# The output bias in a two-layer graph attention kernel: from a matmul to an addition on GpSimd

## The chip, the cores and the metric

The kernel runs on one core of a Trainium2 chip. The metric is device microseconds per execution, the median of three runs. The engines are TensorE (PE; its weight loads are listed as PEld), VectorE (DVE), ScalarE (ACT), GpSimd (POOL) and SyncE (SP), which issues every DMA here. Each engine takes its instructions in the order of its own program and stops at the first whose semaphore has not been reached.

## The reference, cut to what matters

128 graphs of 128 nodes with 512 features go through two layers. Layer 0 is cosine-gated graph attention with 8 heads, and its output is x1. Layer 1 is masked attention with 4 heads of 64, then an output projection with a bias and a residual:

```python
    h = jnp.maximum(_layernorm(x, axis=-1), 0.0)
    x = x + _L0_gnn_ref(h, adj, ...)                 # x1 in the kernel
    h = jnp.maximum(_layernorm(x, axis=-1), 0.0)
    x = x + _L1_gnn_ref(h, adj, ...)                 # ends in: return out @ Wo + bo
```

So the result of a graph is x1 + out @ Wo + bo, with bo (512 values, not zero) the same for all its rows. It must come out in fp32.

## The kernel before, in words

All matrix products are done on fp16 pairs: a value is split into an upper fp16 part (written by ScalarE) and a lower one (the difference, mostly made by GpSimd, some by VectorE). Products are three passes: upper by upper, upper by lower, lower by upper. Projections of layer 0 go over two graphs at a time.

Time is divided into slots, one per graph, and every engine has a function `slot(s)` that lists its work of that slot; odd and even slots differ, so the work repeats every two slots (a pair, in which two graphs are finished). The order is written out by hand, the loops are unrolled, and semaphores alone connect the engines. In slot n the kernel works on graph n of layer 0, graph n-4 and n-3 of layer 1, and the output of graph n-5. The names that the prediction uses:

- POOL, odd slot: `h1_lower` (line 571), `squares_last` (631), `keep_and_block` (618, 625), `x_lower` (602, twice), `o1_lower` (577), `q_lower` (609), `inverse_norms` (a power, 637, and two copies, 643), `q_lower`, `e_lower` (588), `directions_lower` (650, twice), `norm_l1` (659 to 664), `o1_lower`.
- POOL, even slot: `h1_lower`, `v_lower` (594, twice), `keep_and_block`, `p1_lower` (583), `e_lower`, `p1_lower`, `norm_l1`, `norm_l0`.
- SyncE, odd slot: `turn_h1`, two small loads, `turn_x` (transposes what `x_lower` completes, 500, twice), `load_x` (509, twice), `turn_o1` (438, transposes the attention output o_hl into o_t), the two halves of `turn_e`, `store` (490).
- ScalarE, odd slot, after the exponentials: `o1_upper` for the second graph (813), which overwrites o_hl and so waits until `turn_o1` has landed, then the upper part of the first half of k (821), of lq, and `directions_upper` (838, twice), and later the second half of k (821).
- VectorE, odd slot: `k_lower` (966, the lower part of k, both inputs in SBUF), lq's lower part (991), `directions` (1039, twice), the second half of k, `result` (1084).
- PE: in an odd slot `scores`, `cosines`, the projections q, k, lq, lk, the sums, and `output` before lk; in an even slot `scores`, `cosines`, the layer-1 scores, the projections m, the sums, `output`, then v and lv.

`scores` of the next slot waits for `k_lower` of the second half of k, and `cosines` for `directions_lower`. The output is a PSUM bank that PE fills with the bias first, and VectorE scales and adds to x1:

```python
nc.tensor.matmul(ps, three_rows[:, :], bias_y[:, :], start=True, stop=False)
rows(ps, w_o, o_t, first=False).then_inc(proj_full, 1)
```

Here three_rows is 128x128 with ones in rows 0, 32 and 64, and bias_y holds bo over the output scale as a sum of three bf16 parts in those rows, prepared once by eight instructions of GpSimd.

Of the kernel before, what the change touches and what calls it, by code (L numbers as in the profile page):

```python
# [30 lines left out]
BF16 = mybir.dt.bfloat16  # L31
# [8 lines left out]
P = 128  # L40
# [88 lines left out]
def wait(engine, sem, count):  # L129

    if isinstance(count, int) and count <= 0:
        return
    engine.wait_ge(sem, count)
# [21 lines left out]
def build(nc, x, adj, map_w, map_b, q_w, q_b, k_w, k_b, gcn_map_w, gcn_map_b, gcn_W, Wq, Wk, Wv, Wo, bo, out):  # L155
# [13 lines left out]
    with ExitStack() as ctx:  # L169
        def sb(name, shape, dt=F32):  # L170
            return ctx.enter_context(nc.sbuf_tensor(name, shape, dt))

        def sem(name):
            return ctx.enter_context(nc.semaphore(name))
# [9 lines left out]
        w_o = [sb(f"w_o_{s}", [P, C1, D], F16) for s in ("hi", "lo")]  # L184

        ident = sb("ident", [P, P])
        three_rows = sb("three_rows", [P, P], BF16)
        bias_y = sb("bias_y", [P, D], BF16)
        head_sel = sb("head_sel", [P, C, H], BF16)
        minus_half = sb("minus_half", [P, 2 * H])  # L190
        largest = sb("largest", [P, NAMED])
# [5 lines left out]
        v_unscale = sb("v_unscale", [P, 2])  # L197
        v_unkept = sb("v_unkept", [P, 1])
        y_scale = sb("y_scale", [P, 1])
        y_unscale = sb("y_unscale", [P, 1])  # L200
        col_map_b = sb("col_map_b", [P, C])
        col_qb = sb("col_qb", [P, C])
        col_kb = sb("col_kb", [P, C])
# [171 lines left out]
        p1_done = sem("p1_done")  # L375
        dir_hi = sem("dir_hi")
        dir_lo = sem("dir_lo")
        bias_step = sem("bias_step")
        settled_sp = sem("settled_sp")
        settled_pool = sem("settled_pool")  # L380
        settled_dve = sem("settled_dve")
# [18 lines left out]
                + [("gcn", None, 0)] + [("split", w_v, c) for c in range(C)] + [("bias_v", None, 0)]  # L400
                )
        SMALL_LOADS = 7
        ONES = 9
        L_AT = 2 * C
        TURNED_K = 3 * C + 1 + C
        BIAS_K = TURNED_K + C + 1
# [132 lines left out]
        def _(pool):  # L539
# [11 lines left out]


            pool.wait_ge(consts, 7)
            nc.gpsimd.memset(three_rows[:, :], 0.0).then_inc(ones_in, 1)
            nc.gpsimd.memset(lv_sb[:, 0, :, :, DH:DH + 1], 1.0).then_inc(ones_in, 1)
            nc.gpsimd.memset(lv_sb[:, 1, :, :, DH:DH + 1], 0.0).then_inc(ones_in, 1)
            pool.wait_ge(ones_in, 3)
            for part in range(3):
                nc.gpsimd.memset(three_rows[32 * part:32 * part + 1, :], 1.0).then_inc(ones_in, 1)
            pool.wait_ge(ones_in, 6)  # L560
            pool.wait_ge(largest_done, 1)
            nc.gpsimd.partition_all_reduce(top[:, 0:1], largest[:, 0:1], P, RED.absmax).then_inc(top_done, 1)
            pool.wait_ge(largest_done, NAMED)
# [3 lines left out]
            def h1_lower(s):  # L567
                if s.has(-2):
                    pool.wait_ge(h1_hi, s.at(lambda t: t - 2 + 1))
                    a = s.n % 2  # L570
                    nc.gpsimd.tensor_tensor(h1_hl[:, a, 1, :], h1_sb[:, a, :], h1_hl[:, a, 0, :],  # L571
                                            ALU.subtract).then_inc(h1_lo, 1)

            def o1_lower(s, behind):
                if s.has(-behind):
# [52 lines left out]
            def squares_last(s):  # L628
                if s.has(1):
                    pool.wait_ge(sq_rest_done, s.at(lambda t: (t + 1) // 2 + 1))  # L630
                    nc.gpsimd.tensor_tensor(sq_parts[2], sq_rest[:, :, :], sq_parts[1], ALU.subtract).then_inc(sq_last_done, 1)
# [47 lines left out]
            def slot(s):  # L679
                if s.odd:  # L680
                    h1_lower(s)
                    squares_last(s)
                    keep_and_block(s)
                    x_lower(s)
                    o1_lower(s, 5)
                    q_lower(s, 0)
                    inverse_norms(s)
                    q_lower(s, 1)
                    e_lower(s)
                    directions_lower(s, 0)  # L690
                    directions_lower(s, 1)
                    norm_l1(s)
                    o1_lower(s, 4)
                else:
                    h1_lower(s)
                    v_lower(s)
                    keep_and_block(s)
                    p1_lower(s, 4)
                    e_lower(s)
                    p1_lower(s, 3)  # L700
                    norm_l1(s)
                    norm_l0(s)

            early_slots(B, slot)
            pool.wait_ge(scale_done, 2)
            nc.gpsimd.tensor_scalar(bias_o[:, :], bias_o[:, :], y_unscale[:, :], None, ALU.mult).then_inc(bias_step, 1)
            pool.wait_ge(bias_step, 1)
            nc.gpsimd.tensor_copy(bias_y[:, :], bias_o[:, :]).then_inc(bias_step, 1)
            pool.wait_ge(bias_step, 2)
            nc.gpsimd.tensor_tensor(ybuf[:, 0, :], bias_o[:, :], bias_y[:, :], ALU.subtract).then_inc(bias_step, 1)  # L710
            pool.wait_ge(bias_step, 3)
            nc.gpsimd.tensor_copy(bias_y[32:64, :], ybuf[32:64, 0, :]).then_inc(bias_step, 1)
            nc.gpsimd.tensor_copy(bias_y[64:128, :], ybuf[64:128, 0, :]).then_inc(bias_step, 1)
            pool.wait_ge(bias_step, 5)
            nc.gpsimd.tensor_tensor(ybuf[64:128, 1, :], ybuf[64:128, 0, :], bias_y[64:128, :], ALU.subtract).then_inc(bias_step, 1)
            pool.wait_ge(bias_step, 6)
            nc.gpsimd.tensor_copy(bias_y[64:128, :], ybuf[64:128, 1, :]).then_inc(ones_in, 1)
            pool.wait_ge(ones_in, 7)
            pool.wait_ge(prep_copied, BIAS_K)
            nc.gpsimd.memset(v_sb[:, 0, :, :, DK:DK + 1], 1.0).then_inc(ones_in, 1)  # L720
            nc.gpsimd.memset(v_sb[:, 1, :, :, DK:DK + 1], 0.0).then_inc(ones_in, 1)
# [174 lines left out]
        def _(dve):  # L896
# [182 lines left out]
            def result(s):  # L1079
                if s.has(-5):  # L1080
                    u = s.proj("wo")
                    dve.wait_ge(proj_full, u.full)
                    wait(dve, y_out, s.at(lambda t: 16 * (t - 6)))
                    nc.vector.scalar_tensor_tensor(out=ybuf[:, s.n % 2, :], in0=proj_ps[:, u.bank, :], scalar=y_scale[:, 0:1],
                                                   in1=x1[:, (s.n - 5) % 8, :], op0=ALU.mult,
                                                   op1=ALU.add).then_inc(proj_out[u.bank], 1)

            def slot(s):
# [63 lines left out]
            def other_scales():  # L1152
# [9 lines left out]
                for n, (src, _, _, _) in enumerate(st_l):  # L1162
# [25 lines left out]
                                        ALU.mult).then_inc(limit_step, 1)  # L1188
                dve.wait_ge(limit_step, 21)
                nc.vector.scalar_tensor_tensor(out=y_scale[:, :], in0=unscale[:, WO:WO + 1], scalar=H_SCALE,  # L1190
                                               in1=v_unscale[:, 1:2], op0=ALU.mult, op1=ALU.mult).then_inc(limit_step, 1)
                dve.wait_ge(limit_step, 22)
                nc.vector.reciprocal(y_unscale[:, :], y_scale[:, :]).then_inc(scale_done, 1)

            splits = 0
            for u, (kind, dst, part) in enumerate(PREP):
# [31 lines left out]
        def _(pe):  # L1228
# [67 lines left out]
                                               start=n == 0, stop=n == len(passes) - 1)  # L1296
                ins.then_inc(proj_full, 1)

            def rows(ps, w, h, first=True):

                passes = [(i, a, b) for i in range(w[0].shape[1]) for a, b in ((0, 0), (0, 1), (1, 0))]
                for n, (i, a, b) in enumerate(passes):
                    ins = nc.tensor.matmul(ps, h[:, a, i, :], w[b][:, i, :], start=first and n == 0,  # L1303
                                           stop=n == len(passes) - 1)
                return ins

# [86 lines left out]
            def output(s):  # L1393
                if s.has(-5):
                    pe.wait_ge(o1_in, s.at(lambda t: 16 * (t - 5 + 1)))
                    ps = start_proj(s, "wo")
                    nc.tensor.matmul(ps, three_rows[:, :], bias_y[:, :], start=True, stop=False)
                    rows(ps, w_o, o_t, first=False).then_inc(proj_full, 1)

            def m_part(s, half):  # L1400
                if s.has(2):
# [72 lines left out]
```

## Time and profile before

| | us |
|---|---|
| median of 3 runs | 2867.19 (2866.46 to 2871.12) |
| the profiled execution | 2866.04, of which the span is 2864.2 |
| PE busy | 2635.6 (92%) |
| DVE busy | 2011.8 (70%) |
| POOL busy | 1993.1 (70%) |
| ACT busy | 1684.7 (59%) |
| mean granted TensorE clock | 0.972 |

The slices of the page show the same picture from about 200 us to the end: a steady state, in which a pair of slots repeats. The span of PE is read with care: its matmuls overlap, so that their recorded lengths add up to more than they take one behind the other. What a matmul takes in a row of them is read from the chain of waits or from the distance between two starts.

### The profile page before, as it was taken

The page shows a single profiled execution, that of the slowest core. Times are in us where ns is not written, and L with a number is a line of the kernel's source. Part 1 is how long each engine was busy: PE and PEld are TensorE (multiplying, and loading weights), DVE is VectorE, ACT ScalarE, POOL GpSimd, SP SyncE. Part 2 cuts the span into 40 slices and gives each one's busy share as a digit, 9 for nine tenths or more (in the row PEclk, how much of TensorE's full clock was granted, in tenths as well). Part 3 has the DMA queues.
Part 4 walks back from the last instruction along what each step waited for, and adds up shares of the span by engine and source line. Part 5 has one row for each costly group of instructions (what it writes and reads, how often), then busy time and mean ns, then how long its engine had stood idle before and what let it go on. Part 6 is the DMA issues. An engine that isn't in the chain of part 4 may idle for free.

```text
span 2864.2 us, 78990 instructions
## 1 busy us (share of the span) xinstructions
PE 2635.6 (92%) x30809; PEld 2103.3 (73%) x30809; DVE 2011.8 (70%) x3457; ACT 1684.7 (59%) x4501; POOL 1993.1 (70%) x2332
## 2 busy tenths in 40 slices
PE   5789999999999999999999999999999999999985
PEld 3567777777777777777777777777777777777763
DVE  4367777777777777777777777777777777777763
ACT  1256666665666655666665566566556656656653
POOL 0377677677677677777877777787777778767762
PEclk7899999999999999999999999999999999999997
DMA  3145555655555555655655565565566555555543
GB/s 100 35 87 107 102 107 114 104 105 111 103 104 112 111 105 108 118 101 108 114 109 109 105 119 103 105 114 110 101 115 117 102 107 114 110 96 114 113 87 71
DMA packets 829123, 299.08 MB, mean 104 GB/s; under 512 B 772560, under 2 KB 778192, under 8 KB 828752
## 3 DMA queue, kind: packets, MB, share of 16 engines
q1 hardware_dynamic: 828752, 294.04, 53.5%
q8 instruction: 245, 4.01, 0.6%
q14 instruction: 126, 1.03, 0.1%
HBM read 75.80 MB, written 33.55 MB: 38 GB/s over the span
## 4 chain that ended last, share of the span: by engine, by line
PE 54%; POOL 24%; issue 8%; DVE 7%; ACT 3%; DMA 2%; SPq 1%; DVEq 0%; ACTq 0%; POOLq 0%
PE proj_ps L1295 23%; PE proj_ps L1303 18%; POOL inv_norm L637 6%; POOL e_ec L588 4%; POOL dir_hl L650 4%; PE s_ps L1313 4%; PE c_ps L1313 3%; POOL qk_hl L609 2%; POOL inv_rows L643 2%; DVE qk_hl L966 2%; PE mix_ps L1313 2%; ACT qk_hl L821 2%; DMA o_t<-o_hl 2%; PE s_ps L1354 1%; POOL rstd L662 1%
## 5 line engine op out<-in xcount | busy, mean ns | idle before, releaser
L732 ACT ACTIVATE e_ec<-e_ec,neg_mx 128x128 f32<-128x128 f32 x1024 | 396.0, 388 | 4.3
L966 DVE TENSOR_TENSOR qk_hl<-qk_sb,qk_hl 128x512 f16<-128x512 f32 x128 | 125.2, 978 | 355.0 <-ACT qk_hl L821 354.6
L583 POOL TENSOR_TENSOR p_hl<-p_sb,p_hl 128x512 f16<-128x512 f32 x128 | 148.3, 1159 | 314.8 <-ACT p_hl L753 314.8
L1295 PE MATMUL proj_ps<-h_t,w_m_hi 128*128 128x256 f16 x2048 | 350.7, 278 | 9.4 <-DMA h_t<-h_hl 9.4
L1295 PE MATMUL proj_ps<-h_t,w_k_hi 128*128 128x256 f16 x2048 | 344.6, 274 | 0.0
L1295 PE MATMUL proj_ps<-h_t,w_q_hi 128*128 128x256 f16 x2048 | 339.5, 273 | 0.0
L1303 PE MATMUL proj_ps<-w_v_hi,h_t 128*128 128x512 f16 x1024 | 325.4, 379 | 0.0
L588 POOL TENSOR_TENSOR e_ec<-e_ec 128x1024 f16<-128x1024 f32 x128 | 287.2, 2244 | 17.1 <-ACT e_ec L759 17.1
L1295 PE MATMUL proj_ps<-h_t,w_m_lo 128*128 128x256 f16 x1024 | 283.9, 277 | 0.0
L1295 PE MATMUL proj_ps<-h_t,w_k_lo 128*128 128x256 f16 x1024 | 280.1, 274 | 0.0
L1295 PE MATMUL proj_ps<-h_t,w_q_lo 128*128 128x256 f16 x1024 | 279.1, 273 | 0.0
L786 ACT ACTIVATE h_sb<-x,shift,rstd 128x512 f32<-128x512 f32 x128 | 103.4, 808 | 231.5 <-POOL shift L664 231.5
L1313 PE MATMUL s_ps<-qk_hl 64*128 64x128 f16 x3072 | 112.6, 222 | 130.3 <-DVE qk_hl L966 130.3
L1295 PEld LDWEIGHTS proj_ps<-h_t,w_m_hi 128*128 128x128 f16 x2048 | 198.8, 100 | 42.7 <-issue 12.2
L571 POOL TENSOR_TENSOR h_hl<-h_sb,h_hl 128x512 f16<-128x512 f32 x128 | 153.9, 1203 | 104.6 <-ACT h_hl L794 104.6
L1295 PEld LDWEIGHTS proj_ps<-h_t,w_q_hi 128*128 128x128 f16 x2048 | 195.2, 98 | 28.5
L1295 PEld LDWEIGHTS proj_ps<-h_t,w_k_hi 128*128 128x128 f16 x2048 | 196.4, 98 | 21.9
L637 POOL TENSOR_TENSOR inv_norm<-sq_sum,minus_half 128x16 f32<-128x16 f32 x64 | 186.5, 2913 | 26.3 <-DVE sq_sum L1025 26.3
L1313 PEld LDWEIGHTS s_ps<-qk_hl 64*128 64x128 f16 x3072 | 89.7, 97 | 152.2 <-DVE qk_hl L966 148.1
L943 DVE SCALAR_TENSOR_TENSOR qk_sb<-proj_ps,unscale,bias_q 128x512 f32<-128x512 f32 x128 | 96.2, 751 | 144.1 <-PE proj_ps L1295 143.9
L1303 PEld LDWEIGHTS proj_ps<-w_v_hi,h_t 128*128 128x128 f16 x1024 | 100.1, 98 | 128.9 <-DVE m_sb L943 20.2
L1303 PE MATMUL proj_ps<-w_v_lo,h_t 128*128 128x512 f16 x512 | 194.0, 379 | 0.0
(205 smaller groups left out, 7866.9 us busy)
## 6 DMA issues: line engine op xcount, KB each, us to landing
xa<-in_x_dram SPq DMA_DIRECT2D x128, 256.0 KB, 3.5
xres<-in_x_dram SPq DMA_DIRECT2D x128, 256.0 KB, 2.8
out_dram<-ybuf SPq DMA_DIRECT2D x128, 256.0 KB, 2.5
h_t<-h_hl SPq DMA_TRANSPOSE x256, 3.2
ec_t<-e_ec SPq DMA_TRANSPOSE x256, 3.2
adj_in<-in_adj_dram SPq DMA_DIRECT2D x128, 16.0 KB, 2.1
p_t<-p_hl SPq DMA_TRANSPOSE x128, 3.3
o_t<-o_hl SPq DMA_TRANSPOSE x128, 3.8
```

What stands on the lines that cost most here:

```text
L571: nc.gpsimd.tensor_tensor(h1_hl[:, a, 1, :], h1_sb[:, a, :], h1_hl[:, a, 0, :], ALU.subtract).then_inc(h1_lo, 1)
L583: nc.gpsimd.tensor_tensor(p1_hl[:, b, 1], p1_sb[:, b], p1_hl[:, b, 0], ALU.subtract).then_inc(p1_lo, 1)
L588: nc.gpsimd.tensor_tensor(e_hl[:, 1], e_sb[:, :, :], e_hl[:, 0], ALU.subtract).then_inc(e_lo, 1)
L637: nc.gpsimd.tensor_tensor(inv_norm[:, :], sq_sum[:, :], minus_half[:, :], ALU.pow).then_inc(inv_norm_done, 1)
L650: nc.gpsimd.tensor_tensor(dir_hl[:, 1, :, cols], m_sb[:, :, cols], dir_hl[:, 0, :, cols], ALU.subtract).then_inc(dir_lo, 1)
L732: ins = nc.scalar.activation(e[:, h, :], e[:, h, :], ACT.Exp, bias=neg[:, h:h + 1], scale=SCALE, accum_out=sums[:, h:h + 1])
L786: nc.scalar.activation(h1_sb[:, a, :], x1[:, (s.n - 1) % 8, :], ACT.Relu, bias=shift1[:, 0:1], scale=rstd1[:, 0:1]).then_inc(h1_done, 1)
L943: nc.vector.scalar_tensor_tensor(out=dst[:, c0:c0 + 2, :], in0=proj_ps[:, u.bank, :].rearrange("p (c n) -> p c n", c=2), scalar=factor, in ...
L966: nc.vector.tensor_tensor(k_hl[:, 1, c, :], k_sb[:, c, :], k_hl[:, 0, c, :], ALU.subtract).then_inc(k_lo, 1)
L1295: ins = nc.tensor.matmul(out, w[a][:, i, c * P:(c + 1) * P], h[:, :, b, i, :], start=n == 0, stop=n == len(passes) - 1)
L1303: ins = nc.tensor.matmul(ps, h[:, a, i, :], w[b][:, i, :], start=first and n == 0, stop=n == len(passes) - 1)
L1313: ins = nc.tensor.matmul(outs[half][c], st[r, a, c, cols], mv[r, b, c, cols], start=n == 0, stop=n == 2)
```

## The change

The bias matmul, its two operands and their preparation are gone. A new function of GpSimd, `result_base`, writes x1 + bo into the output buffer at the head of each slot that has an output, behind `h1_lower`. It takes over the wait for the store that last used this buffer, and VectorE's `result` now waits for the new semaphore y_base and reads the buffer that it writes in place of x1.

```diff
+            def result_base(s):
+                if s.has(-5):
+                    wait(pool, y_out, s.at(lambda t: 16 * (t - 6)))
+                    settle(pool, settled_pool, s.i)
+                    nc.gpsimd.tensor_tensor(ybuf[:, s.n % 2, :], x1[:, (s.n - 5) % 8, :], bias_o[:, :],
+                                            ALU.add).then_inc(y_base, 1)
...
             def slot(s):
                 if s.odd:
                     h1_lower(s)
+                    result_base(s)
                     squares_last(s)
...
                 else:
                     h1_lower(s)
+                    result_base(s)
                     v_lower(s)
...
             pool.wait_ge(scale_done, 2)
-            nc.gpsimd.tensor_scalar(bias_o[:, :], bias_o[:, :], y_unscale[:, :], None, ALU.mult).then_inc(bias_step, 1)
...
-            nc.gpsimd.tensor_copy(bias_y[64:128, :], ybuf[64:128, 1, :]).then_inc(ones_in, 1)
-            pool.wait_ge(ones_in, 7)
...
                     dve.wait_ge(proj_full, u.full)
-                    wait(dve, y_out, s.at(lambda t: 16 * (t - 6)))
+                    dve.wait_ge(y_base, s.at(lambda t: t - 4))
                     nc.vector.scalar_tensor_tensor(out=ybuf[:, s.n % 2, :], in0=proj_ps[:, u.bank, :], scalar=y_scale[:, 0:1],
-                                                   in1=x1[:, (s.n - 5) % 8, :], op0=ALU.mult,
+                                                   in1=ybuf[:, s.n % 2, :], op0=ALU.mult,
                                                    op1=ALU.add).then_inc(proj_out[u.bank], 1)
...
-                dve.wait_ge(limit_step, 22)
-                nc.vector.reciprocal(y_unscale[:, :], y_scale[:, :]).then_inc(scale_done, 1)
...
                     ps = start_proj(s, "wo")
-                    nc.tensor.matmul(ps, three_rows[:, :], bias_y[:, :], start=True, stop=False)
-                    rows(ps, w_o, o_t, first=False).then_inc(proj_full, 1)
+                    rows(ps, w_o, o_t).then_inc(proj_full, 1)
```

On POOL, at the head of an odd slot in the steady state, the order before was:

```order
L571 TENSOR_TENSOR h_hl<-h_sb,h_hl 128x512
L631 TENSOR_TENSOR sq_t<-sq_rest 128x1024
L618 TENSOR_SCALAR keep<-adj_in,v_unkept,v_unscale 128x1
L625 TENSOR_SCALAR block<-adj_in 128x128
L602 TENSOR_TENSOR h_hl<-xa,h_hl 128x512 x2
L577 TENSOR_TENSOR o_hl<-o_sb,o_hl 128x256
```

and the same place of the changed kernel (its lines have other numbers) is:

```order
L563 TENSOR_TENSOR h_hl<-h_sb,h_hl 128x512
L570 TENSOR_TENSOR ybuf<-x,bias_o 128x512
L630 TENSOR_TENSOR sq_t<-sq_rest 128x1024
L617 TENSOR_SCALAR keep<-adj_in,v_unkept,v_unscale 128x1
L624 TENSOR_SCALAR block<-adj_in 128x128
L601 TENSOR_TENSOR h_hl<-xa,h_hl 128x512 x2
L576 TENSOR_TENSOR o_hl<-o_sb,o_hl 128x256
```

One addition of 128x512 (`ybuf<-x,bias_o`) now stands ahead of both `x_lower`s, whose results SyncE waits for. In an even slot it stands at the same place, ahead of the two `v_lower`s.

On PE, in an even slot, the output's bank was begun by the bias matmul, between the weighted sums and the projection:

```order
L1354 MATMUL s_ps<-v_sb,ec_t 128x65 x24
L1397 MATMUL proj_ps<-bias_y,three_rows 128x512
L1303 MATMUL proj_ps<-w_o_hi,o_t 128x512
L1303 MATMUL proj_ps<-w_o_lo,o_t 128x512
L1303 MATMUL proj_ps<-w_o_hi,o_t 128x512 x2
```

and is now begun by the projection itself:

```order
L1340 MATMUL s_ps<-v_sb,ec_t 128x65 x24
L1289 MATMUL proj_ps<-w_o_hi,o_t 128x512
L1289 MATMUL proj_ps<-w_o_lo,o_t 128x512
L1289 MATMUL proj_ps<-w_o_hi,o_t 128x512 x2
```

Nothing else on PE has moved: one matmul of 512 columns is gone in each of the 128 slots that have an output.

## Rows read from the trace of the kernel before

**Rows 1.** The page: the span, and section 4, engines on the chain that ended last.

```profile
span 2864.2 us, 78990 instructions
...
PE 54%; POOL 24%; issue 8%; DVE 7%; ACT 3%; DMA 2%; SPq 1%; DVEq 0%; ACTq 0%; POOLq 0%
```

**Rows 2.** The chain of waits, 1490 to 1580 us: start us, us, what.

```profile
1517.98 0.84 PE s_ps L1313 x24
...
1526.24 0.22 PE proj_ps L1397
```

**Rows 3.** The same view from 2760 us, at the end of the run.

```profile
2857.82 0.61 PE proj_ps L1397
```

**Rows 4.** Groups by line and form: busy us, mean ns, idle before, releaser.

```profile
L1397 PE MATMUL proj_ps<-bias_y,three_rows 128*128 128x512 bf16 x128 | 49.5, 386 | 19.5 <-DMA o_t<-o_hl 9.9 <-DVE lq_hl L991 9.5
...
L710 POOL TENSOR_TENSOR ybuf<-bias_o,bias_y 128x512 f32<-128x512 f32 x1 | 1.2, 1152 | 0.1
```

**Rows 5.** POOL's timeline, 1490 to 1580 us: start us, us, line, operation, [idle before].

```profile
1494.38 1.16 POOL L571 TENSOR_TENSOR h_hl<-h_sb,h_hl 128x512 f16<-128x512 f32 x1
1495.49 1.90 POOL L631 TENSOR_TENSOR sq_t<-sq_rest 128x1024 bf16<-128x1024 f32 x1
...
1498.17 2.28 POOL L602 TENSOR_TENSOR h_hl<-xa,h_hl 128x512 f16<-128x512 f32 x2
1501.94 0.68 POOL L577 TENSOR_TENSOR o_hl<-o_sb,o_hl 128x256 f16<-128x256 f32 x1 [1.49 <-ACT o_hl L813]
...
1504.17 2.91 POOL L637 TENSOR_TENSOR inv_norm<-sq_sum,minus_half 128x16 f32<-128x16 f32 x1 [0.44 <-DVE sq_sum L1025]
...
1509.47 2.58 POOL L588 TENSOR_TENSOR e_ec<-e_ec 128x1024 f16<-128x1024 f32 x1
1512.06 2.27 POOL L650 TENSOR_TENSOR dir_hl<-m_sb,dir_hl 128x512 f16<-128x512 f32 x2
...
1527.37 1.16 POOL L583 TENSOR_TENSOR p_hl<-p_sb,p_hl 128x512 f16<-128x512 f32 x1 [4.76 <-ACT p_hl L753]
```

**Rows 6.** SyncE's timeline, 1490 to 1545 us (issues of DMAs).

```profile
1499.36 2.67 SPq L500 DMA_TRANSPOSE h_t<-h_hl  x2
1502.08 2.06 SPq L509 DMA_DIRECT2D xa<-in_x_dram  x2
1504.23 1.20 SPq L438 DMA_TRANSPOSE o_t<-o_hl  x1
...
1518.62 0.35 SPq L490 DMA_DIRECT2D out_dram<-ybuf  x1
```

**Rows 7.** ScalarE's timeline of the same stretch.

```profile
1507.59 0.42 ACT L813 ACTIVATE o_hl<-o_sb 128x256 f16<-128x256 f32 x1 [3.04 <-DMA o_t<-o_hl]
```

**Rows 8.** VectorE's timeline of the same stretch.

```profile
1508.56 1.50 DVE L966 TENSOR_TENSOR qk_hl<-qk_sb,qk_hl 128x512 f16<-128x512 f32 x1 [1.11 <-ACT qk_hl L821]
```

**Rows 9.** POOL's timeline in another pair, 1619 to 1646 us.

```profile
1628.37 2.91 POOL L637 TENSOR_TENSOR inv_norm<-sq_sum,minus_half 128x16 f32<-128x16 f32 x1 [0.43 <-DVE sq_sum L1025]
...
1633.67 2.12 POOL L588 TENSOR_TENSOR e_ec<-e_ec 128x1024 f16<-128x1024 f32 x1
1638.34 2.27 POOL L650 TENSOR_TENSOR dir_hl<-m_sb,dir_hl 128x512 f16<-128x512 f32 x2 [2.54 <-ACT dir_hl L838]
```

**Rows 10.** ScalarE's timeline in that pair.

```profile
1633.14 0.42 ACT L813 ACTIVATE o_hl<-o_sb 128x256 f16<-128x256 f32 x1 [4.39 <-DMA o_t<-o_hl]
```

**Rows 11.** VectorE's timeline in that pair.

```profile
1634.12 2.23 DVE L966 TENSOR_TENSOR qk_hl<-qk_sb,qk_hl 128x512 f16<-128x512 f32 x1 [2.46 <-ACT qk_hl L821]
```

**Rows 12.** Line 650 on POOL: what ended its idle before it (us, times).

```profile
  ACT dir_hl L838: 23.4, 10
```

**Rows 13.** POOL's timeline, 1410 to 1480 us: two starts of the power.

```profile
1420.03 2.91 POOL L637 TENSOR_TENSOR inv_norm<-sq_sum,minus_half 128x16 f32<-128x16 f32 x1 [0.44 <-DVE sq_sum L1025]
...
1462.86 2.91 POOL L637 TENSOR_TENSOR inv_norm<-sq_sum,minus_half 128x16 f32<-128x16 f32 x1 [0.43 <-DVE sq_sum L1025]
```

**Rows 14.** Stretch 1433 to 1440 us: five engines' busy us, PEclk, DMA share, GB/s.

```profile
1433.00:1440.00 7.00, 6.16 (x95) 5.34 (x96) 5.64 (x7) 3.54 (x15) 3.94 (x5) 0.76 0.70 101
```

More of the change, by code:

```diff
@@ L186, in build @@
         ident = sb("ident", [P, P])
-        three_rows = sb("three_rows", [P, P], BF16)
-        bias_y = sb("bias_y", [P, D], BF16)
         head_sel = sb("head_sel", [P, C, H], BF16)
@@ L199, in build @@
         y_scale = sb("y_scale", [P, 1])
-        y_unscale = sb("y_unscale", [P, 1])
         col_map_b = sb("col_map_b", [P, C])
@@ L377, in build @@
         dir_lo = sem("dir_lo")
-        bias_step = sem("bias_step")
+        y_base = sem("y_base")
         settled_sp = sem("settled_sp")
@@ L402, in build @@
         SMALL_LOADS = 7
-        ONES = 9
+        ONES = 4
         L_AT = 2 * C
@@ L553, in _ @@
             pool.wait_ge(consts, 7)
-            nc.gpsimd.memset(three_rows[:, :], 0.0).then_inc(ones_in, 1)
             nc.gpsimd.memset(lv_sb[:, 0, :, :, DH:DH + 1], 1.0).then_inc(ones_in, 1)
             nc.gpsimd.memset(lv_sb[:, 1, :, :, DH:DH + 1], 0.0).then_inc(ones_in, 1)
[L557 to L560, printed above, removed]
             pool.wait_ge(largest_done, 1)
@@ L705, in _ @@
             pool.wait_ge(scale_done, 2)
-            nc.gpsimd.tensor_scalar(bias_o[:, :], bias_o[:, :], y_unscale[:, :], None, ALU.mult).then_inc(bias_step, 1)
[L707 to L716, printed above, removed]
-            nc.gpsimd.tensor_copy(bias_y[64:128, :], ybuf[64:128, 1, :]).then_inc(ones_in, 1)
-            pool.wait_ge(ones_in, 7)
             pool.wait_ge(prep_copied, BIAS_K)
@@ L1190, in other_scales @@
                 nc.vector.scalar_tensor_tensor(out=y_scale[:, :], in0=unscale[:, WO:WO + 1], scalar=H_SCALE,
-                                               in1=v_unscale[:, 1:2], op0=ALU.mult, op1=ALU.mult).then_inc(limit_step, 1)
-                dve.wait_ge(limit_step, 22)
-                nc.vector.reciprocal(y_unscale[:, :], y_scale[:, :]).then_inc(scale_done, 1)
+                                               in1=v_unscale[:, 1:2], op0=ALU.mult, op1=ALU.mult).then_inc(scale_done, 1)
             splits = 0
@@ L1297, in features, with rows @@
                 ins.then_inc(proj_full, 1)
-            def rows(ps, w, h, first=True):
+            def rows(ps, w, h):
                 passes = [(i, a, b) for i in range(w[0].shape[1]) for a, b in ((0, 0), (0, 1), (1, 0))]
                 for n, (i, a, b) in enumerate(passes):
-                    ins = nc.tensor.matmul(ps, h[:, a, i, :], w[b][:, i, :], start=first and n == 0,
+                    ins = nc.tensor.matmul(ps, h[:, a, i, :], w[b][:, i, :], start=n == 0,
                                            stop=n == len(passes) - 1)
```

## The prediction

> **What bounds the kernel now.** I read the page first, then the chain of waits, then the four timelines of one pair of slots, and then the same timelines in a pair that took longer. The span is 2864.2 us; on the chain PE has 54% and POOL 24% [rows 1]. So PE alone does not set the end, and an exchange of PE work for POOL work has to be priced place by place. In the steady state a pair takes 41.3 us (from 1462.86 to 1504.17, two starts of the power that makes the inverse norms [rows 5, 13]). Through the even slot and the first third of the odd one the chain is PE's, without a gap. Then VectorE sums the squares, and from 1504.17 POOL carries the chain: power, two copies, q_lower, e_lower, two directions_lower, the layer-1 norm; ScalarE and VectorE finish k, and PE starts the next scores at 1517.98 [rows 2, 5], having idled for about 2 us.
>
> A second path joins this one with nothing to spare. POOL's x_lower (1498.17) lets SyncE turn x from 1499.36; SyncE then issues two loads at 1502.08 and the transpose of o at 1504.23 [rows 5, 6]. Only when that has landed may ScalarE overwrite o_hl, at 1507.59 [rows 7]; behind it in ScalarE's order stands the upper part of k, and for that VectorE's k_lower waits, which starts at 1508.56, 4.39 us after the power began [rows 5, 8]. From there: lq, directions, ScalarE's upper part, POOL's directions_lower at 1512.06, just as e_lower ends [rows 5].
>
> This path has a cliff. k_lower takes 1.50 us here [rows 8] and 2.23 us in the pair at 1628 [rows 11]. In the first it came while POOL's q_lower ran, ran after it, and POOL's e_lower, at 1509.47, waited for it (2.58 us instead of 2.12 [rows 5, 9]). In the second the transpose landed later (ScalarE at 1633.14), k_lower came at 1634.12, 0.45 us behind the start of e_lower at 1633.67, and ended at 1636.35, after e_lower's end at 1635.79; directions_lower then started 9.97 us after the power instead of 7.89 [rows 5, 9 to 11]. So being late for e_lower's start costs 2.08 us, however little late it is. e_lower starts 5.30 us after the power. POOL's waits for ScalarE before directions_lower are 23.4 us in 10 [rows 12]: one of 0.5 in the preparation, and nine such pairs of 2.54. Going through all pairs, k_lower is behind e_lower's start in exactly these nine.
>
> The Trainium skill (SBUF — State Buffer, Who interferes with whom) says that a VectorE instruction with two SBUF inputs and a GpSimd instruction that reads SBUF exclude each other, and that whoever issues first blocks the other for its whole length; by that rule the step is a cliff, and without it a slope. The trace agrees, with the 2.23 us of a k_lower that takes about 0.6 after e_lower's end [rows 9, 11].
>
> The clock adds to it. In the stretch from 1433 to 1440, after PE's idle, the granted clock averages 0.76, that is, half of it at the lower level of 1.2 GHz and the rest at 2.4 [rows 14], and that pair takes 42.83 us (1420.03 to 1462.86) instead of 41.3: 1.5 us more [rows 13]. This happens behind 6 of the nine late pairs, where PE idles about 4 us, and behind 10 of the other 53.
>
> **The change, part by part.** The sum is made against the profiled execution, 2866.04 us; the median is 1.15 above.
>
> *Removed from PE:* 128 matmuls. Their recorded mean is 386 ns [rows 4], but on the chain one takes 0.22 us [rows 2], since matmuls overlap. In the 64 even slots it is on the chain: 64 x 0.22 = 14.1 us gained, and the power of the odd slot starts 0.22 earlier against the start of the pair. In the odd slots PE waits for POOL anyway; there the matmul only lengthens the idle before the scores. At the end of the run the last outputs are on the chain at the lower clock (0.61 for the first of them [rows 3], of which I take 0.43 as its own time): with the preparation's one VectorE reciprocal, 1.9 us gained.
>
> *Removed from POOL's preparation:* eight short instructions that stand before a longer idle of POOL. Nothing.
>
> *Added on POOL, even slots:* one addition. The nearest row is a tensor_tensor of the same shape and types, 1152 ns recorded [rows 4]; from start to start one of 128x512 takes 1.11 (1494.38 to 1495.49 [rows 5]), which I use. Behind it are v_lower, keep and block, and then 4.76 us of idle before 1527.37 [rows 5]. It is hidden there: nothing. Without that cover it would be 64 x 1.1 = 70 us.
>
> *Added on POOL, odd slots:* the same 1.11 us, ahead of squares_last, keep, block and x_lower. On POOL itself it ends in the idle of 1.49 before o1_lower at 1501.94 [rows 5], so the power is not delayed. But x_lower is, by 1.11, and SyncE waits for it: turn_x, both loads and the transpose of o go out 1.11 later. SyncE has no gap between them in which to take that back (1499.36, 1502.08, 1504.23 [rows 6]), and the transpose lands behind the loads' data. k_lower therefore comes 1.11 later against the start of the pair, and 1.11 + 0.22 = 1.33 later against the power: at 4.39 + 1.33 = 5.72 in the pair shown, beyond 5.30. Over the 60 pairs in which all of this runs, 49 lie beyond 5.30 when shifted by 1.33, if the landing keeps its spread. But it has a memory: behind a late pair the transpose lands about 1 us sooner, and of the nine pairs behind a late one only 3 would be late when shifted. With a chance of 49/60 or a little more behind an ordinary pair and 3/9 behind a late one, 34 are late. Between 34 and 49 I take 42: 33 more than now, 33 x 2.08 = 68.6 us. The clock: 42 x 6/9 + 20 x 10/53 = 32 pairs instead of 16, 16 x 1.5 = 24 us.
>
> *Waits.* The wait for the store moves to POOL's head of slot, where all of POOL's slot is queued behind it. The store of the same buffer goes out at 1518.62 [rows 6], and the addition comes about 18 us later: nothing. VectorE's wait for y_base is for something done some 20 us before; its own instruction still has one operand in PSUM and one in SBUF: nothing, with at most 0.05 x 128 = 6 us either way.
>
> *Sum:* 2866.0 - 14.1 - 1.9 + 68.6 + 24 = 2942.6, and 1.2 more for the median: 2944 us. With 34 late pairs it is 52 + 19.5 - 16 = 55 more than now (2922), with 49 it is 83 + 28 - 16 = 95 more (2962).
>
> **The rivals.**
> 1. *The addition is hidden, PE's gain stays.* If the landing of the transpose is set by other traffic and moves by less than 0.9 us, a typical pair stays this side of 5.30 (4.39 + 0.9). Then 14.1 + 1.9 are gained: 2851. For it: the landings spread by over a microsecond with SyncE's issues at the same place. Against it: the transpose stands behind loads that SyncE issues only after x_lower. It decides from a shift of 0.9 downwards.
> 2. *Nearly every pair is late.* If the late pairs' memory is gone when all are shifted, 62 are late: 53 x 2.08 = 110, the clock (41 - 16) x 1.5 = 37.5, less 16: 2999. For it: 49 of 60 already at the old spread. Against it: the sooner landing behind late pairs.
> 3. *No cliff, only a shift.* If k_lower were not blocked by e_lower, it would end at 5.72 + 0.6 = 6.3 instead of 5.89 after the power (1508.56 + 1.50 [rows 8]), and directions_lower start 0.4 later: 64 x 0.4 - 16 = +10, 2877. Against it stands the pair at 1628.
> 4. *Nothing changes*, because some late pairs more (6 or 7 at 2.08, plus clock) just cancel the 16 us: 2867.
>
> **How the numbers follow.** A difference under 0.2% (5.7 us) can't be told from none here. Forecast (between 30 and 55 late pairs) 0.58; rival 1 0.14; rival 2 0.16; rival 3 0.07; rival 4 0.05. Faster is rival 1, same is rival 4, slower the rest: 0.14, 0.05, 0.81. The likeliest case's own range is 2912 to 2975. The range of 8 in 10 leaves out most of rival 1 and 4 below and little above: 2868 to 3000.
>
> **What would show it.** In the changed kernel's profile: (a) POOL's new line takes about 1.15 us recorded, 128 times; its wait for the store is nothing. (b) SyncE's turn of x starts 1.1 later against the pair's start, and ScalarE's wait for the transpose of o grows from 3.0 us by about 1 in ordinary pairs. (c) POOL waits before directions_lower in some 42 pairs, about 2.5 us each, 100 us in all instead of 23.4; (d) PE's wait for k_lower before the scores grows; the mean clock falls a little. (e) Ordinary pairs take 41.15 us, 0.22 less than before, late ones 43.2, and with the clock 44.7. The prediction is wrong if the waits of (c) stay at ten: then the transpose did not move, and rival 1 holds. It is wrong in its size if the number of late pairs is outside 30 to 55, or if the even slots' addition delays v_lower or block enough to be waited for.

## The result

The changed kernel takes 2937.38 us (median of 4 runs, 2930.47 to 2944.54) against 2866.82 for the kernel before on the same occasions: a ratio of 1.0244, 95% interval 1.0217 to 1.0271. It is slower by about 70 us; the forecast was 2944.

The page of the changed kernel, its span, engines' busy time and the engines on the chain that ended last. Against [rows 1] PE has lost 9 points of the chain and POOL 4, though POOL's busy time has grown from 1993.1 to 2123.8 us; VectorE, ScalarE, SyncE and the DMAs have more of it than before (12%, 6%, 3% and 5% against 7%, 3%, 1% and 2%):

```profile
span 2936.8 us, 78851 instructions
...
PE 2628.8 (90%) x30681; PEld 2105.9 (72%) x30681; DVE 2036.3 (69%) x3456; ACT 1681.6 (57%) x4501; POOL 2123.8 (72%) x2449
...
PE 45%; POOL 20%; DVE 12%; issue 9%; ACT 6%; DMA 5%; SPq 3%; ACTq 0%; DVEq 0%; POOLq 0%
```

The waits of the whole run (engine, line, what it waited for: us in total, times, longest). The third row answers to [rows 12]: GpSimd now waits 41 times for ScalarE's directions_upper instead of 10, one of them in the preparation in either kernel, 102.4 us instead of 23.4. The first is the wait of [rows 7], 4.1 us on average:

```profile
ACT o_hl L801 <- DMA o_t<-o_hl: 261.3, 64, 6.0
...
PE s_ps L1299 <- DVE qk_hl L954: 155.0, 64, 4.5
...
POOL dir_hl L649 <- ACT dir_hl L826: 102.4, 41, 2.6
```

One late pair on GpSimd's timeline (start us, us, line, operation, idle before), to be laid beside [rows 5, 9]. The addition (L570) stands between h1_lower and squares_last and takes 1.24 us from start to start. The power starts at 1583.19, e_lower 5.30 later, directions_lower 9.97 later:

```profile
1574.36 1.27 POOL L570 TENSOR_TENSOR ybuf<-x,bias_o 128x512 f32<-128x512 f32 x1
1575.60 1.89 POOL L630 TENSOR_TENSOR sq_t<-sq_rest 128x1024 bf16<-128x1024 f32 x1
...
1578.27 2.27 POOL L601 TENSOR_TENSOR h_hl<-xa,h_hl 128x512 f16<-128x512 f32 x2
...
1583.19 2.92 POOL L636 TENSOR_TENSOR inv_norm<-sq_sum,minus_half 128x16 f32<-128x16 f32 x1 [0.43 <-DVE sq_sum L1013]
...
1588.49 2.13 POOL L587 TENSOR_TENSOR e_ec<-e_ec 128x1024 f16<-128x1024 f32 x1
1593.16 2.27 POOL L649 TENSOR_TENSOR dir_hl<-m_sb,dir_hl 128x512 f16<-128x512 f32 x2 [2.54 <-ACT dir_hl L826]
```

SyncE in the same pair. Its turn of x starts 3.74 us before the power, where it had been 4.81 before it (1499.36 against 1504.17 in [rows 5, 6]):

```profile
1579.45 2.60 SPq L497 DMA_TRANSPOSE h_t<-h_hl  x2
1582.11 1.05 SPq L506 DMA_DIRECT2D xa<-in_x_dram  x2
1583.26 1.19 SPq L435 DMA_TRANSPOSE o_t<-o_hl  x1
```

This pair and the one of [rows 5, 6] must not be compared by the transpose of o (the last row here) alone: it goes out 0.07 us after the power here and 0.06 after it there, because there the two loads took SyncE 2.06 us to issue, and here 1.05, as in most pairs. Over the 60 pairs counted below it goes out 0.79 us ahead of the power before the change and 0.58 behind it after, so 1.37 later on average. From there to ScalarE's o1_upper, which waits for it, it takes 4.28 us on average before and 3.98 after: landing sooner takes back a part, and o1_upper is 1.07 later. Which pairs are late is decided more by this last stretch than by the issue: in the changed kernel it is 4.23 us on average in the late ones against 3.48 in the others, and 5.60 against 4.04 before, where the issue itself differs by less than 0.2 us.

In the pair shown o1_upper starts 5.60 us after the power instead of 3.42 [rows 7]:

```profile
1588.79 0.42 ACT L801 ACTIVATE o_hl<-o_sb 128x256 f16<-128x256 f32 x1 [5.22 <-DMA o_t<-o_hl]
```

VectorE: k_lower comes 1.27 us behind the start of e_lower and ends at 1591.17, 0.55 us behind e_lower's end at 1590.62:

```profile
1589.76 1.41 DVE L954 TENSOR_TENSOR qk_hl<-qk_sb,qk_hl 128x512 f16<-128x512 f32 x1 [3.29 <-ACT qk_hl L809]
```

Where the 70 us went, counted over the 60 pairs of the steady state in the two profiled executions. A pair runs from one power to the next. It is late when directions_lower starts more than 9 us after the power. It "has the lower clock" when it is over 1 us longer than its like; the mean granted clock is 0.96 in each of these pairs and 1.00 in every other. An ordinary pair is neither late nor has the lower clock.

| | before | changed |
|---|---|---|
| late pairs | 9 | 40 |
| pairs with the lower clock | 16 | 29 |
| late pairs that have the lower clock | 6 of 9 | 27 of 40 |
| what the lower clock adds to a pair, mean | 1.43 us | 1.20 us |
| an ordinary pair, median | 41.38 us | 41.39 us |
| mean start of the turn of x, against the power | -4.86 us | -3.65 us |
| mean issue of the transpose of o, against the power | -0.79 us | 0.58 us |
| mean start of ScalarE's o1_upper, against the power | 3.49 us | 4.56 us |
| late pairs among those that follow a late one / another | 1 of 9 / 8 of 50 | 24 of 40 / 15 of 19 |
| first to last power | 2638.0 us | 2716.2 us |
| rest of the span | 226.2 us | 220.6 us |

31 late pairs more at 2.08 us are 64.5 us. The lower clock cost 16 x 1.43 = 23 us before and costs 29 x 1.20 = 35 now, 12 more (why a pair pays less for it now is said below, with PE's gain). Together that is 76.5 of the 78.2 us by which the steady state has grown. The ends gave back 5.6 us, and 72.6 remain between the two profiled executions.

### The profile page after: what moved, and what is told of

It reads as the page before. It is cut to its first block, busy times and chain, and to the rows that moved or that the text cites. A ratio compares the mean times of both kernels' runs of the same rounds, so it can differ in the third digit from the quotient of the medians.

```text
span 2936.8 us, 78851 instructions
## 1 busy us (share of the span) xinstructions
PE 2628.8 (90%) x30681; PEld 2105.9 (72%) x30681; DVE 2036.3 (69%) x3456; ACT 1681.6 (57%) x4501; POOL 2123.8 (72%) x2449
## 4 chain that ended last, share of the span: by engine, by line
PE 45%; POOL 20%; DVE 12%; issue 9%; ACT 6%; DMA 5%; SPq 3%; ACTq 0%; DVEq 0%; POOLq 0%
PE proj_ps L1281 20%; PE proj_ps L1289 13%; DVE qk_hl L954 4%; DMA o_t<-o_hl 4%; POOL dir_hl L649 4%; PE s_ps L1299 3%; PE c_ps L1299 3%; POOL inv_norm L636 2%; ACT qk_hl L809 2%; POOL h_hl L601 2%; POOL e_ec L587 2%; PE mix_ps L1299 2%; POOL sq_t L630 2%; SPq L497 1%; POOL rstd L661 1%
## 5 line engine op out<-in xcount | busy, mean ns | idle before, releaser
L954 DVE TENSOR_TENSOR qk_hl<-qk_sb,qk_hl 128x512 f16<-128x512 f32 x128 | 152.3, 1190 | 425.3 <-ACT qk_hl L809 425.3
L1299 PE MATMUL s_ps<-qk_hl 64*128 64x128 f16 x3072 | 123.9, 235 | 155.0 <-DVE qk_hl L954 155.0
L1299 PEld LDWEIGHTS s_ps<-qk_hl 64*128 64x128 f16 x3072 | 99.1, 103 | 176.9 <-DVE qk_hl L954 172.8
L1289 PE MATMUL proj_ps<-w_o_hi,o_t 128*128 128x512 f16 x512 | 174.9, 383 | 52.2 <-DVE lq_hl L979 42.7
L649 POOL TENSOR_TENSOR dir_hl<-m_sb,dir_hl 128x512 f16<-128x512 f32 x128 | 145.2, 1155 | 102.5 <-ACT dir_hl L826 102.4
L801 ACT ACTIVATE o_hl<-o_sb 128x256 f16<-128x256 f32 x128 | 52.3, 409 | 264.6 <-DMA o_t<-o_hl 261.3
```

The costliest lines, as they stand in the source:

```text
L649: nc.gpsimd.tensor_tensor(dir_hl[:, 1, :, cols], m_sb[:, :, cols], dir_hl[:, 0, :, cols], ALU.subtract).then_inc(dir_lo, 1)
L954: nc.vector.tensor_tensor(k_hl[:, 1, c, :], k_sb[:, c, :], k_hl[:, 0, c, :], ALU.subtract).then_inc(k_lo, 1)
L1299: ins = nc.tensor.matmul(outs[half][c], st[r, a, c, cols], mv[r, b, c, cols], start=n == 0, stop=n == 2)
```

## The experiments

Each group ran beside the kernel before on one chip, and ratios are against it. The kernel before itself took 2854 to 2860 us there; the number of late pairs differs from execution to execution (9 in its own profile, 3 to 10 in those of the kernels below whose transpose goes out as before), and only ratios of one group are compared.

**The addition behind the x_lowers.**

```diff
                     h1_lower(s)
-                    result_base(s)
                     squares_last(s)
                     keep_and_block(s)
                     x_lower(s)
+                    result_base(s)
```

> The changed kernel with one line moved: in odd slots GpSimd's addition stands behind the two x_lowers instead of ahead of them; same work on every engine. Theory 1 (the addition costs only because SyncE's turn of x, its loads and the transpose of o wait for x_lower, and k_lower then falls behind e_lower's start): the addition now fills 1.2 of the 1.5 us in which GpSimd waits for o1_upper, the transpose goes out as before, late pairs fall from 40 back to about 9 of 60, GpSimd's waits before directions_lower from 102 us to about 25, and the time is 2867 less what the missing matmul gives (4 to 16): 2850 to 2863. Theory 2 (GpSimd carries a quarter of the chain, so its 128 x 1.2 us cost wherever they stand): 2930 or more.

Measured: 2851.13 us, ratio 0.9985 (0.9967 to 1.0004). GpSimd's timeline shows the addition (L570) between x_lower and o1_lower, and 0.27 us of idle left of 1.49 [rows 5]:

```profile
1524.56 2.27 POOL L601 TENSOR_TENSOR h_hl<-xa,h_hl 128x512 f16<-128x512 f32 x2
1526.79 1.27 POOL L570 TENSOR_TENSOR ybuf<-x,bias_o 128x512 f32<-128x512 f32 x1
1528.33 0.67 POOL L576 TENSOR_TENSOR o_hl<-o_sb,o_hl 128x256 f16<-128x256 f32 x1 [0.27 <-ACT o_hl L801]
```

Its wait for directions_upper in the whole run (POOL waits, us in total, times) says that late pairs are down to 3:

```profile
POOL dir_hl L649 <- ACT dir_hl L826: 8.1, 4, 2.5
```

The work is the same as in the changed kernel on every engine, and the whole loss is gone: the 64 additions of the odd slots, 1.2 us each, cost nothing where nobody waits behind them. Theory 2 has fallen.

**Only the matmul gone.**

```diff
-                    nc.tensor.matmul(ps, three_rows[:, :], bias_y[:, :], start=True, stop=False)
-                    rows(ps, w_o, o_t, first=False).then_inc(proj_full, 1)
+                    rows(ps, w_o, o_t).then_inc(proj_full, 1)
```

> The kernel before without the bias matmul and with nothing in its place; this leaves the output bias out of the result (the preparation of its operands stays). It measures PE's part alone. By the prediction's term 14 us in the even slots and 2 at the end are gained: 2851. By the trace of the changed kernel, where PE's v projection then waits 0.18 us for VectorE's m_features and ordinary pairs still take 41.38 us, only 0.07 x 62 = 4 and 2 to 4 at the end are gained: 2859 to 2862. Late pairs stay near 9, perhaps a few more, since the matmul in the odd slot also only moves PE.

Measured (the result lacks the output bias): 2846.76 us, ratio 0.9973 (0.9957 to 0.9989), so 8 us less with an interval of 3 to 12. In its profile 5 pairs are late and an ordinary pair takes 41.38 us, no less than with the matmul. But a pair that has the lower clock and is not late takes 42.62 us (9 pairs), where in the kernel before it takes 42.83 (10 pairs).

**Only the addition, in odd or in even slots.** Ahead of squares_last in odd slots, or ahead of the v_lowers in even ones:

```diff
+                    nc.gpsimd.tensor_tensor(spare[:, 0:D], x1[:, (s.n - 5) % 8, 0:D], bias_o[:, 0:D], ALU.add)
```

> The kernel before, bias matmul kept, with one extra GpSimd addition of 128x512 fp32 (x1 + bo into a spare tile that nobody reads) behind h1_lower in odd slots only, where the changed kernel has it. Theory 1: the whole loss and more, since no matmul is saved: about 40 of 60 pairs late, 2867 + 31 x 2.08 + 13 x 1.4 = 2950 (2935 to 2965). Theory 2: 64 x 1.2 = 77 is 2944, not told apart by the time alone but by the pairs: all longer by 1.2 instead of some by 2.1 or 3.5.

> The kernel before, bias matmul kept, with the same extra GpSimd addition behind h1_lower in even slots only. Theory 1: hidden in 4.8 us of idle before p1_lower: 2867 within 5, late pairs about 9 of 60. Theory 2: 64 x 1.2 = 77 us more, 2944.

Measured: in odd slots 2937.23 us, ratio 1.0286 (1.0248 to 1.0324); in even slots 2857.93 us, ratio 1.0017 (0.9995 to 1.0039), where the interval leaves room for up to 11 us. The odd ones alone make 35 of 60 pairs late, ordinary pairs staying at 41.39; with the even ones alone 10 are late. POOL's wait with the odd ones:

```profile
POOL dir_hl L655 <- ACT dir_hl L844: 89.6, 36, 2.5
```

**Half the addition.** The same in odd slots, of 256 columns.

> As the run with the extra addition in odd slots only, but of 128x256: about 0.7 us instead of 1.2 ahead of x_lower, matmul kept, result into a spare tile. Theory 1 (a cliff at e_lower's start): each pair is either undisturbed or late by 2.08; k_lower's starts in the kernel before, shifted by 0.7, lie beyond 5.30 us in about 20 to 25 of 60, less a few for the memory, so 15 to 25 late pairs instead of 35, each still directions_lower at 9.97; time 1.010 to 1.018 of before. Theory 3 (a slope, each pair later by the shift beyond some slack): all pairs late by the same few tenths, directions_lower at 8.0 to 8.6, none at 9.97.

Measured: 2890.31 us, ratio 1.0107 (1.0085 to 1.0128). The turn of x starts 0.68 us later than before; 19 pairs are late, and directions_lower starts 7.8 to 8.0 or 10.0 us after the power in all 60, never between. What ended POOL's idle before line 655 (us, times):

```profile
  ACT dir_hl L844: 48.8, 20
```

A little more than half the delay gives 19 late pairs where the whole delay gave 35, each at the full price. That is a cliff and not a slope.

**e_lower in two halves.**

```diff
-                    nc.gpsimd.tensor_tensor(e_hl[:, 1], e_sb[:, :, :], e_hl[:, 0], ALU.subtract).then_inc(e_lo, 1)
+                    for h in range(0, H, H // 2):
+                        ins = nc.gpsimd.tensor_tensor(e_hl[:, 1, h:h + H // 2], e_sb[:, h:h + H // 2, :],
+                                                      e_hl[:, 0, h:h + H // 2], ALU.subtract)
+                    ins.then_inc(e_lo, 1)
```

> The changed kernel with GpSimd's e_lower in two instructions of 128x512 in place of one of 128x1024, in both kinds of slot. Theory 1 with exclusion (k_lower, when it comes while e_lower runs, waits for that whole instruction): a k_lower that comes during the first half gets in after it, at 6.4 us instead of 7.4 after the power, and the second half then waits 0.6; directions_lower starts about 9.0 instead of 9.97. Most late pairs cost 1.1 instead of 2.1: 1.010 to 1.016 of before instead of 1.024. Theory 4 (VectorE and GpSimd share the bandwidth, k_lower is only slowed): no change beyond 0.1 us per pair, 1.024.

Measured: 2908.70 us, ratio 1.0177 (1.0151 to 1.0203), better than 1.0244 but outside the 1.010 to 1.016 expected. GpSimd in a typical pair:

```profile
1569.13 2.92 POOL L639 TENSOR_TENSOR inv_norm<-sq_sum,minus_half 128x16 f32<-128x16 f32 x1 [0.43 <-DVE sq_sum L1016]
...
1574.44 2.72 POOL L588 TENSOR_TENSOR e_ec<-e_ec 128x512 f16<-128x512 f32 x2
1578.14 2.27 POOL L652 TENSOR_TENSOR dir_hl<-m_sb,dir_hl 128x512 f16<-128x512 f32 x2 [0.98 <-ACT dir_hl L829]
```

VectorE's k_lower there. It came 0.70 us after the first half had begun and ended at 1576.14, where the first half's length (about 1.1 us) plus its own 0.56 puts it; it did not wait for the whole e_lower:

```profile
1575.14 1.00 DVE L957 TENSOR_TENSOR qk_hl<-qk_sb,qk_hl 128x512 f16<-128x512 f32 x1 [2.73 <-ACT qk_hl L812]
```

Directions_lower starts 9.01 us after the power. Over the 60 pairs it starts at 8.0 to 8.1 in 21, at 9.0 to 9.1 in 36 and at 10.1 in 3: the step is halved. In the three at 10.1 k_lower came 6.5 us or more after the power, when the second half had begun, and missed both. The time fell less than the step because ordinary pairs grew by 0.1 us (two instructions, 2.28 instead of 2.13) and 27 of the 36 pairs at 9.0 to 9.1 still had the lower clock.

**Two buffers for o_hl**, in the changed kernel and in the kernel before (the index that picks the buffer stands wherever o_hl is written or turned):

```diff
-                    wait(act, o1_in, s.at(lambda t: 16 * (t - behind)))
-                    nc.scalar.activation(o_hl[:, 0, :], o1_sb[:, :], ACT.Copy).then_inc(o1_hi, 1)
+                    wait(act, o1_in, s.at(lambda t: 16 * (t - behind - 1)))
+                    nc.scalar.activation(o_hl[:, (s.n - behind) % 2, 0, :], o1_sb[:, :], ACT.Copy).then_inc(o1_hi, 1)
```

> The changed kernel with two buffers for o_hl, so that ScalarE's o1_upper no longer waits for the transpose that was issued just before (it waits for the one before that); the addition stays ahead of x_lower. Theory 1: SyncE's transpose is still issued 1.2 us later, but nothing on ScalarE hangs on it; k_lower starts near 3 us after the power, no pair is late, GpSimd never waits 2.5 us before directions_lower, pairs take 41.3, or 42.8 with the lower clock: all of the loss gone and the nine late pairs of before too, 0.985 to 0.995 of before. Theory 2 (GpSimd's own time): no change, 1.02 of before.

> The kernel before (bias matmul kept) with two buffers for o_hl and nothing else. Theory 1: its own few late pairs (3 to 10 of 60) are gone, some 10 to 25 us less, 0.990 to 0.996 of before; with the run of the changed kernel with two buffers it says what the exchange of matmul for addition is worth once the transpose is off the path: 4 to 8 us in favour of the addition.

Measured: 2820.85 us, ratio 0.9865 (0.9843 to 0.9887), and 2820.36 us, ratio 0.9864 (0.9845 to 0.9882). The second is lower than the 0.990 to 0.996 expected; the last section says where the rest came from. In the first, SyncE still issues the transpose late, at 1520.39 with the power at 1520.16:

```profile
1519.24 1.06 SPq L507 DMA_DIRECT2D xa<-in_x_dram  x2
1520.39 1.19 SPq L436 DMA_TRANSPOSE o_t<-o_hl  x1
```

ScalarE writes the next o_hl at once (second row; no idle for a DMA), and k_lower starts 3.0 to 3.4 us after the power in every pair:

```profile
1517.46 0.40 ACT L802 ACTIVATE o_hl<-o_sb 128x256 f16<-128x256 f32 x1
...
1520.45 0.40 ACT L802 ACTIVATE o_hl<-o_sb 128x256 f16<-128x256 f32 x1
1522.65 0.63 ACT L810 ACTIVATE qk_hl<-qk_sb 128x512 f16<-128x512 f32 x1 [1.81 <-DVE qk_sb L932]
```

GpSimd's idle before directions_lower (us, times) is gone but for one in the preparation, so the addition's place has lost its price together with this one link:

```profile
  ACT dir_hl L827: 0.5, 1
```

The exchange itself, with the transpose off the path, is worth nothing: 2820.85 against 2820.36, where 4 to 8 us were expected. All 60 pairs are ordinary ones, and they take 41.34 us with the addition and 41.33 with the matmul.

**Where PE's 0.22 us go.** In even slots, m_features ahead of l1_max on VectorE, on top of the two buffers:

```diff
-                    l1_max(s, 3)
                     m_features(s, 1)
+                    l1_max(s, 3)
```

> The changed kernel with two buffers for o_hl, and in even slots VectorE's second m_features ahead of the second l1_max. It asks where PE's 0.22 us per pair went. Theory 5 (PE's v projection waits for the bank that m_features empties, and VectorE reaches m_features just when PE would have finished the output with its bias matmul, so a shorter output only waits): with m_features 0.68 us earlier PE goes on at once, ordinary pairs take 41.15 instead of 41.36, PE's wait for m_features is gone, and the time is about 13 us below the same kernel without the swap (2820.85 there): 0.981 to 0.984 of before. Theory 6 (the gain is lost at another place, as GpSimd's or ScalarE's chain of the even slot): no gain from the swap, 0.9865.

> The same two edits on the kernel before, which keeps its bias matmul. Theory 5: the swap alone gives 0 to 4 us here, since PE is busy with the output until VectorE is done anyway: 0.985 to 0.987 of before, some 10 us above the run without the matmul. Theory 6: equal to the run without the matmul.

> The two edits, and the addition of odd slots behind the x_lowers, as the candidate for the best version. Once the transpose is off the path the addition's place should not matter: within 3 us of the run with the addition ahead of them. If SyncE's delay by 1.2 us still cost something elsewhere (the turned x, the loads), it would be lower by more.

Measured: 2819.22 (ratio 0.9858, 0.9834 to 0.9882), 2814.45 (0.9837, 0.9809 to 0.9865) and 2818.18 (0.9850, 0.9826 to 0.9875). By their intervals the three can't be told apart, and the one that keeps its matmul has the lowest median and not the highest. Theory 5 in this form has failed: PE's wait for m_features is gone, but an ordinary pair takes 41.29 us without the matmul and 41.30 with it, and nothing more has come of the missing matmul. The place of the addition doesn't matter here, as expected. The chain of waits of the first one shows what holds PE now: L1073 is VectorE's result, and PE's lv projection starts when it has emptied the bank:

```profile
1502.48 0.67 DVE ybuf L1073
1503.15 0.05 issue
1503.19 5.38 PE proj_ps L1290 x36
```

**result ahead of attended** on VectorE in even slots, on top of it:

```diff
-                    attended(s)
                     result(s)
+                    attended(s)
```

> The run with two buffers for o_hl and m_features first, with one more exchange on VectorE in even slots: result (which empties the output's bank) ahead of attended. In the run before this one PE's lv projection began 0.05 us after result had ended. Theory 7 (PE's gain in the even slot is held by VectorE through two banks: m_features for v, result for lv): with both freed about 1.9 us earlier PE runs on, an ordinary pair takes 41.1 to 41.2 instead of 41.3, and the time is 6 to 13 us below that run, 0.981 to 0.984 of before. Theory 8 (it is held by a chain without banks, such as GpSimd's norm or the exponentials, which attended later by 0.7 us would lengthen): no gain, or up to 20 us of loss.

Measured: 2800.56 us (2793.33 to 2801.86), ratio 0.9794 (0.9767 to 0.9821), 19 us below the kernel without this exchange (2819.22, in the group before) where 6 to 13 were expected. An ordinary pair takes 40.99 us. PE's output, v and lv projections of the even slot now run as one piece of 54 matmuls, without a wait for VectorE:

```profile
1531.12 0.73 PE s_ps L1341 x24
1531.84 9.10 PE proj_ps L1290 x54
```

This is the best version: 59 us (2.1%) below the kernel before, which took 2859.93 us beside it, with the bias added by GpSimd. What it would take with the matmul kept was not run.

## Why the prediction was right, and where it was not

*The path through SyncE, and that POOL's own odd slot absorbs the addition:* right. x_lower, turn of x, loads and transpose moved together, the power did not move against POOL's own work, and the move of one line or of one buffer takes the whole loss away. This is shown by four runs: the addition behind x_lower, the two with additions in odd or even slots, and two buffers.

*The cliff:* right, in place (5.30 us after the power), price (2.08) and kind. The halved addition shows the step, the halved e_lower that its height is the length of the GpSimd instruction that k_lower meets.

*The even slots' addition hidden:* right, 1.0017 with an interval that holds 1.

*The number of late pairs:* 42 of 62 expected from the spread and the memory, 40 of 60 found. The memory was weaker than the nine pairs of before suggested: behind a late pair 24 of 40 are late again, not 3 of 9. The shift was smaller in return. The prediction moved k_lower by 1.33 us with the landing's spread kept; the turn of x moved by 1.21 (the addition takes 1.23 and not 1.11 from start to start, and the 0.22 of the matmul did not come), the transpose goes out 1.37 later, but it lands sooner after its issue, and o1_upper moved by 1.07. Two errors met; the count was nearer than it had a right to be. Why the transpose lands sooner is not shown.

*The clock:* 32 pairs expected, 29 found; of the late pairs 27 of 40 against the 6 of 9 taken. The price was 1.20 us a pair and not 1.5, so the term was 12 us and not 24.

*PE's gain of 14.1 us in the even slots: this step failed.* The prediction took the 0.22 us off the chain of waits, since the matmul stood on it, and named nothing that would be late next. Ordinary pairs take as long as before. In the changed kernel's chain, PE ends the output and then waits for VectorE's m_features, which empties the bank that v is to be written to (a piece of the chain between two powers 41.38 apart):

```profile
1499.11 2.93 POOL inv_norm L636
...
1521.95 0.67 DVE m_sb L931
1522.62 0.05 issue
1522.66 7.97 PE proj_ps L1289 x48
...
1540.49 2.93 POOL inv_norm L636
```

The kernel before had said so, in rows that the prediction did not weigh. Waits of its weight loads for the two VectorE instructions that empty the output's neighbours, each in 44 pairs:

```profile
PEld proj_ps L1303 <- DVE m_sb L943: 20.2, 44, 0.5
...
PEld proj_ps L1303 <- DVE ybuf L1084: 11.9, 44, 0.3
```

In the chain of the kernel before PE ended the output at 1527.75 and began v 0.03 us later, so VectorE and PE were level within a tenth of a microsecond and a shorter PE only waited:

```profile
1526.46 1.29 PE proj_ps L1303 x6
1527.78 7.97 PE proj_ps L1303 x48
```

The count of these waits says where the matmul did matter. 44 are the 60 pairs less the 16 with the lower clock, and pair by pair it is just those: every pair at the full clock has both waits, no pair with the lower clock has either. It is the same in the changed kernel (31 of 60, 29 with the lower clock):

```profile
PEld proj_ps L1289 <- DVE m_sb L931: 20.8, 31, 0.7
```

and in the kernel with only the matmul gone (49 of 60, 11 with the lower clock):

```profile
PEld proj_ps L1303 <- DVE m_sb L943: 33.1, 49, 0.7
```

With the lower clock PE is the later of the two, and there the missing matmul shortens a pair: one that is not late takes 42.62 us instead of 42.83, a late one 44.68 instead of 44.9 (27 pairs of the changed kernel against 20 of the kernel with additions in odd slots). So PE's gain was about 0.2 us in 29 pairs, some 6 us, and not 0.22 in 64; it is in the 1.20 us by which the lower clock is now priced. For the removal alone this gives 11 to 16 pairs x 0.2 = 2 to 3 us, and in its profile the ends are 4.4 us shorter (221.8 against 226.2): about 7 in all, within the 3 to 12 us measured.

Freeing the first bank alone gave 0.05 us per ordinary pair (41.34 to 41.29), freeing both another 0.3 (40.99): two gates in a row hold like one until both are open. What the missing matmul by itself is worth behind them stays open, since the run with the matmul kept and both gates open was not made.

*The ends:* 1.9 us expected, 5.6 found (1.6 ahead of the first power and 4.0 behind the last).

*The sum:* the forecast's terms were 68.6 for late pairs, 24 for the clock, 14.1 off for PE and 1.9 off at the ends, 76.6 us in all. Found were 64.5, 12, nothing in ordinary pairs and 5.6 off: 71 by these prices, and 72.6 by the spans. Late pairs and clock were put 16 us too high, and PE's gain 14 too high with the other sign, so the errors cancelled; that the forecast came within 7 us is luck in part. (In the case of 34 late pairs the prediction took 19.5 us for the clock; its own rule gives 12 pairs x 1.5 = 18. It doesn't change the range.)

## What to carry to other kernels

Before work is put into an engine's idle time, follow what the instructions behind it release, not only whether the engine itself has time: here the addition fitted into 1.5 us of idle, but it stood ahead of a producer that a DMA queue was waiting for, and at the end of that queue was a buffer. When instructions of two engines exclude each other, as k_lower and e_lower do here, look for the margin with which the shorter one gets in, since beyond it the price is the other's whole length (2.08 us for a GpSimd instruction of 2.13). And when a step is taken off the chain of waits, first find the wait that is late next; waits of a few tenths that occur in most rounds, on weight loads too, are such a margin already used up. It is worth asking which rounds lack them, for those are the ones that a shorter step can still shorten.

## What the runs showed of the hardware that was not expected

With two buffers for o_hl no pair of 60 had the lower clock, in the profile of any of the kernels, against 16 of 60 before; the mean granted clock over the whole run was 0.980 to 0.983 against 0.972. PE still idles before the scores in every pair, 110 us in all with the matmul and 122.5 without it, against 130.3 before. The prediction had taken the lower clock in ordinary pairs as a matter of chance; with regular pairs it did not occur at all, and it gives about as much of the gain as the late pairs themselves (16 x 1.43 = 23 us beside 9 x 2.08 = 19; the steady state of the kernel before shrank by 43.8 us, from 2638.0 to 2594.2). What it is in a regular pair that keeps the clock is not shown.

The addition with fp32 output takes 1.27 us recorded and 1.23 from start to start, where the tensor_tensor of the same shape with fp16 output takes 1.16 and 1.11, and the fp32 one of the preparation had been recorded with 1.152 [rows 4].
